# VectorE takes over the weighing of one-hots for odd blocks in every stage after the first

## The reference

```
x = x + attention(layernorm(x), ctx)          # 16 heads of 16, biases, softmax over 512 keys
x = x + experts(layernorm(x))
experts(x): x_norm = x * rsqrt(mean(x*x) + eps) * norm_w
            q   = x_norm @ wq                 # 8 heads x 2 halves x 128
            sim = q . keys                    # 64 scores per head and half
            top 16 of each half, top 16 of the 256 sums  -> 16 experts of 4096 per head, 128 per token
            hidden = gelu(x_norm . down[expert]) * relu(score)
            out    = sum over experts of hidden * up[expert]
```

## Time and profile before

| | |
|---|---|
| median of 3 runs | 1311.65 us (1310.05 to 1319.98) |
| profiled execution | 1311.6 us, span 1309.8 us |
| PE busy | 1086.9 us, 83% |
| DVE (VectorE) busy | 1038.1 us, 79% |
| POOL (GpSimd) busy | 588.6 us, 45% |
| ACT (ScalarE) busy | 394.9 us, 30% |

### The profile page before, as it was taken

One profiled execution on the slowest core, in us unless ns is written; L12 is line 12 of the kernel. 1 busy time (PEld: TensorE's weight loads), 2 busy tenths in 40 slices (PEclk: granted clock), 3 DMA queues, 4 the chain that ended last, 5 costly groups with the idle time before them and its releaser, 6 DMA issues.

```text
span 1309.8 us, 28838 instructions
## 1 busy us (share of the span) xinstructions
PE 1086.9 (83%) x10152; PEld 741.6 (57%) x10152; DVE 1038.1 (79%) x4899; ACT 394.9 (30%) x724; POOL 588.6 (45%) x708
## 2 busy tenths in 40 slices
PE   4799987887778862458889889998989898989998
PEld 2344442333213221357767778777878777768887
DVE  2657455959998998599999999999989999974621
ACT  1257544533334450122212222222222222222211
POOL 5230410513112123156766767666757575765500
PEclk9699998987879896559999989998999999989999
DMA  4344314221211101800000100010000010000000
GB/s 153 102 150 135 108 51 132 69 71 48 77 45 39 46 15 37 306 4 2 24 6 20 32 10 24 2 32 15 24 11 24 2 32 15 24 9 28 2 17 9
DMA packets 59924, 63.76 MB, mean 49 GB/s; under 512 B 6882, under 2 KB 56164, under 8 KB 59268
## 3 DMA queue, kind: packets, MB, share of 16 engines
q1 hardware_dynamic: 59780, 61.90, 14.8%
HBM read 42.21 MB, written 19.66 MB: 47 GB/s over the span
## 4 chain that ended last, share of the span: by engine, by line
DVE 38%; PE 24%; POOL 16%; issue 15%; DMA 3%; SPq 2%; ACT 2%; POOLq 0%; DVEq 0%; ACTq 0%
PE bank L1242 22%; POOL mem L774 5%; DVE mem L1199 4%; DVE mem L1165 4%; POOL mem L662 3%; DVE mem L1101 3%; DVE mem L1212 3%; PE bank L1245 2%; DVE mem L1084 2%; DVE mem L1097 2%; DVE mem L1104 2%; DVE mem L1196 2%; DVE mem L1048 2%; DVE mem L1047 2%; SPq L487 2%
## 5 line engine op out<-in xcount | busy, mean ns | idle before, releaser
L1242 PE MATMUL bank<-mem 128*128 128x32 bf16 (+5 forms) x9672 | 1037.4, 279 | 151.3 <-issue 60.9
L1242 PEld LDWEIGHTS bank<-mem 128*128 128x128 bf16 (+3 forms) x9672 | 689.3, 125 | 448.8 <-issue 227.6
L774 POOL TENSOR_TENSOR mem<-mem 128x1536 bf16<-128x1536 bf16 x118 | 326.4, 2767 | 249.2 <-DVE mem L1199 216.9
L1165 DVE TENSOR_REDUCE mem<-bank 128x1 f32<-128x512 f32 x256 | 167.8, 681 | 91.0 <-PE bank L1242 90.7
L874 ACT ACTIVATE mem<-bank 128x512 f32<-128x512 f32 x256 | 148.9, 601 | 207.3 <-PE bank L1242 206.4
L1212 DVE TENSOR_TENSOR mem<-mem 128x512 f32<-128x512 f32 x128 | 126.6, 989 | 80.9 <-ACT mem L911 73.5
L911 ACT ACTIVATE mem<-bank 128x512 f32<-128x512 f32 x128 | 76.5, 598 | 341.7 <-PE bank L1242 341.7
L1199 DVE TENSOR_TENSOR mem<-mem 128x2048 bf16<-128x2048 bf16 x128 | 158.9, 1241 | 0.0
L1245 PE MATMUL bank<-mem 128*128 128x128 f32 (+3 forms) x480 | 75.8, 289 | 68.3 <-POOL mem L693 25.0
L662 POOL TENSOR_TENSOR mem<-mem 128x32 f32<-128x32 f32 (+5 forms) x224 | 73.8, 364 | 117.8 <-DVE mem L1056 117.8
L920 ACT COPY mem<-bank 128x512 f32<-128x512 f32 x128 | 74.9, 586 | 160.5 <-PE bank L1242 160.5
(11 more groups left out here) (99 smaller groups left out, 729.2 us busy)
## 6 DMA issues: line engine op xcount, KB each, us to landing
mem<-parts_d SPq DMA_DIRECT2D x192, 64.0 KB, 2.2
parts_d<-mem SPq DMA_DIRECT2D x16, 384.0 KB, 2.6
mem<-in_L_ffn_expert_down SPq DMA_DIRECT2D x16, 256.0 KB, 3.0
downT_d<-mem SPq DMA_DIRECT2D x16, 256.0 KB, 3.1
mem<-downT_d SPq DMA_DIRECT2D x4, 1024.0 KB, 9.9
mem<-in_L_ffn_expert_up SPq DMA_DIRECT2D x4, 1024.0 KB, 17.3
tok_d<-mem SPq DMA_DIRECT2D x16, 160.0 KB, 1.8
mem<-tok_d SPq DMA_DIRECT2D x16, 160.0 KB, 2.5
```

Of the source, the lines that this page charges most:

```text
L774: nc.gpsimd.tensor_tensor(ow[q % 2], i0, i1, ALU.mult).then_inc(ow_rdy, 1)
L1165: nc.vector.tensor_reduce(nmx[g % 2][:, i % TB, i // TB:i // TB + 1], psum[n % 3][:, :], AX.X, ALU.max, negate=True).then_inc(s_max, 1)
L1242: return nc.tensor.matmul(o, l, r, start=first, stop=last)
```

## The change

In stages 0 to 6 VectorE weighs the blocks with odd q and GpSimd those with even q. Stage -1 keeps its division. That makes 56 weighings that move, 8 in each of seven stages. VectorE does its weighing right behind the one-hots of the same block and ahead of the tasks of the step. The address helper and the size are the same as before. `block_weighed` is rewritten to take stage and block apart, so that TensorE, VectorE and SyncE wait on the count to which a block now belongs; no wait is added to any of these queues, except that VectorE waits for its own low one-hots before it weighs them.

```diff
-        OWN = [q for q in range(16) if q % 3 != 0]
-        def block_weighed(eng, c):
-            if isinstance(c, int) and c in OWN:
-                eng.wait_ge(ow_own, OWN.index(c) + 1)
-            elif isinstance(c, int) and c < 16:
-                if c >= 0:
-                    eng.wait_ge(ow_rdy, c + 1 - sum(o < c for o in OWN))
-            else:
-                eng.wait_ge(ow_rdy, c + (1 - len(OWN)))
+        OWN_FIRST = [q for q in range(16) if q % 3 != 0]
+        OWN = [q for q in range(16) if q % 2 != 0]
+        def own(kk, q):
+            return q in (OWN_FIRST if kk == -1 else OWN)
+        def block_weighed(eng, slot, q):
+            if q < 0:
+                slot, q = slot - 1, q + 16
+            if isinstance(slot, int) and slot < 0:
+                return
+            if isinstance(slot, int) and slot == 0:
+                mine = sum(o <= q for o in OWN_FIRST)
+                first, more = mine, q + 1 - mine
             else:
+                mine = sum(o <= q for o in OWN)
+                first, more = len(OWN_FIRST) + mine - len(OWN), 16 - len(OWN_FIRST) + q + 1 - mine - (16 - len(OWN))
+            if own(-1 if isinstance(slot, int) and slot == 0 else 0, q):
+                eng.wait_ge(ow_own, first if isinstance(slot, int) and slot == 0 else slot * len(OWN) + first)
+            else:
+                eng.wait_ge(ow_rdy, more if isinstance(slot, int) and slot == 0 else slot * (16 - len(OWN)) + more)
...
# GpSimd's step
-                    if on(kk, -1, 6) and not (kk == -1 and q in OWN):
+                    if on(kk, -1, 6) and not own(kk, q):
                         weigh((k + 1) * 16 + q, par, q)
...
# VectorE's one_hots
-                block_weighed(dve, c - 2)
+                block_weighed(dve, k + 1, q - 2)
...
-                if kk == -1 and q in OWN:
+                if own(kk, q):
                     dve.wait_ge(oh_rdy, c * 2 + 1)
                     i0, i1 = weighing(q, tt)
                     nc.vector.tensor_tensor(ow[q % 2], i0, i1, ALU.mult).then_inc(ow_own, 1)
...
# TensorE's coefficients
-                block_weighed(pe, c)
+                block_weighed(pe, k + 1, q)
```

More of the change, by code:

```diff
@@ L575, in load_choice @@
                 if isinstance(tile, int):
-                    block_weighed(sp, (tile - 3) * BPT - 1)
-                    block_weighed(sp, (tile - 3) * BPT - 2)
+                    last = (tile - 3) * BPT - 1
+                    block_weighed(sp, last // 16, last % 16)
+                    block_weighed(sp, (last - 1) // 16, (last - 1) % 16)
                 sp.wait_ge(tok_wr, (tile + 1) * 16)
```

## The result

The changed kernel takes 1319.46 us (median of 5 runs, 1316.42 to 1324.21) against 1312.95 us for the kernel before on the same occasions (5 runs, 1310.05 to 1319.98). The ratio is 1.0054, 95% interval 1.0030 to 1.0078: half a per cent slower. The forecast was 1316.8 us, which is 1.0039 of the median of 1311.65 us that it was built on; the measured median is 2.7 us above it, and the measured ratio 0.0015. The profiled execution after takes 1316.4 us, span 1314.5.

What follows compares the result with a forecast made beforehand. The prediction took VectorE to bound stages 0 to 5, with TensorE not far behind. 41.3 - 26.9 - 2.6 - 5.3 - 3.3 + 2 = +5.2 us, on 1311.65 us, gave 1316.8 us, range 1306 to 1325.

Steps and rivals of the forecast that it cites:

- The bound: Stages 0 to 5: VectorE sets the pace, so added work is paid at once; in stage 6 it isn't.
- The added term: Stages 0 to 5: 48 weighings on VectorE at 0.86 us each, +41.3 us; the eight of stage 6 cost nothing.
- The holds by odd blocks: Stages 0 to 5: VectorE instructions stretched while GpSimd weighs odd blocks are no longer held, -26.9 us.
- The waits of `choose`: Three of ten waits for GpSimd's sums stand behind an odd weighing and go, -2.6 us; the long ones stay.
- The waits of `keys`: Four waits of 1.32 us for expert numbers that GpSimd starts late because of an odd weighing go, -5.3 us.
- Even weighings that start late: Where keys follow in an even step, the even weighing starts up to 1.3 us earlier: -3.3 us for four places.
- Disturbance: GpSimd's small operations run beside VectorE's one-hots more often, stretching them: +2 us, between 0 and +6.
- What was to be seen after: Profile: 66 and 62 weighings, multiply some 82 us, line 1084 about half, its waits gone, VectorE busy some 26 us more.
- sign of being wrong: Multiply's gelu waits over 10 us before stage 6, shrinking even holds, or a VectorE weighing clearly over 0.95 us.
- Rival 1: Stages 2 to 5: returned holds become waits for TensorE's gelus; 1337.5 us if all, 1327 if half; chance 0.2.
- Rival 2: GpSimd's free time shortens even holds too: 1304 us if half go, 1288 if all; chance 0.12.
- Rival 3: The port pair shared by VectorE and GpSimd is the bound: 91 us would go, to 1221 us; chance 0.02.

Runs made afterwards that it cites:

- the doubled weighing: Changed kernel plus a second, unused weighing of the same size before each VectorE weighing after stage -1: 1356.64 us in one run.
- the 52 blocks: Against the kernel before, VectorE weighs only 52 blocks of stages 0 to 5 whose GpSimd weighing held or delayed something: 0.9739, 1276.14 us.
- the account: Table over six profiled kernels: length of stages 0 to 5, holds, small stretches, idle, and price per moved weighing, 0.86 to 0.89 us.
- the slice: Kernel before with GpSimd weighing only 64 of 1536 elements per block after stage -1: 1239.93 us in one run.
- even -1.1%: VectorE weighs the even instead of the odd blocks in stages 0 to 6, against the kernel before: 0.9891, 1302.09 us.
- all -0.5%: VectorE weighs every block in stages 0 to 6 and GpSimd none, against the kernel before: 0.9952, 1305.30 us.
- its mirror image: VectorE weighs the other 44 blocks of stages 0 to 5, GpSimd all of stage 6, against the kernel before: 1.0278, 1350.67 us.

## Why the prediction was right, point by point

**The bound.** Right. In stages 0 to 5 VectorE paid every microsecond added (the doubled weighing) and kept every one returned (the 52 blocks). The moved weighings of stage 6 cost nothing: stages 6 and after are 0.8 us shorter.

**The added term.** 48 x 0.86 = 41.3; the account says 0.89 and 42.6. Right to 1.3 us.

**The holds by odd blocks.** -26.9, and the account has no hold by an odd block left. Right.

**The waits of `choose`.** Mis-sized: -2.6 forecast, 17.5 to 11.3 us measured, -6.2. I had said that the long waits all stand behind even blocks. The one of stage 1 stands behind block 3: 3.0 us more. The other 0.6 us are three short waits that stay and fall from 0.86 to 0.67 us.

**The waits of `keys`.** Mis-sized the other way: -5.3 forecast, 5.3 to 3.2 us measured. Only one of four went, that of stage 0, whose numbers stood behind odd block 11; the others fell from 1.32 to 1.06 us. Here the prediction read its rows wrongly. In these three places the weighing just before the numbers is an even one (block 12 of stage 1, block 6 of stages 2 and 4; in the earlier trace rows the one at 821.26), and it stays with GpSimd. The numbers still start 0.13 us ahead of VectorE's next high one-hots (825.11 and 825.24 in the earlier trace rows, 828.87 and 829.00 below). VectorE now has a weighing to do before it needs them, which alone would have shortened the wait by some 0.9 us, but GpSimd takes 0.7 us longer over them: the seven instructions of line 675 took 2.85 us in the earlier trace rows, and at the same place in stage 2, with VectorE's one-hots and weighing beside them, 3.57:

```profile
828.87 3.57 POOL L688 TENSOR_TENSOR mem<-mem 128x128 int32<-128x128 int32 x7
829.00 1.44 DVE L1212 TENSOR_TENSOR mem<-mem 128x2048 bf16<-128x2048 bf16 x1
830.36 1.06 DVE L1218 TENSOR_TENSOR mem<-mem 128x1536 bf16<-128x1536 bf16 x1
832.47 0.57 DVE L1097 SCALAR_TENSOR_TENSOR mem<-mem 128x400 f32<-128x400 f32 x1 [1.06 <-POOL mem L688]
```

**Even weighings that start late.** -3.3 forecast, -0.4 measured (31.7 to 31.3 us of holds by even blocks). A keys step is four two-input instructions in a row, and a weighing that misses the first catches the third, as at 896.40 above: in the timelines the even holds of the keys fell by only 2.4 us (14.4 to 12.0). Those of the multiply, which I had taken to stay, rose by 1.8 (14.4 to 16.2; the 15.5 of the prediction has some 1 us of smaller stretches in it).

**Disturbance.** +2 forecast; the small stretches fell by 1.9 us. What is booked here and what under the added term depends on the duration that is taken as unstretched; together the two terms were +43.3 forecast and +40.7 measured.

So the terms were off by +1.3, -3.6, +3.2, +2.9 and -3.9 us, and it is luck that these cancel: the sign and the size of the two large terms were read from rows, the small ones were right only in sum. By stage the forecast was about +4, near 0, and within 1 in each of the last four; measured are +3.0, -1.4, +2.5, -0.7, +2.5, -0.7. Stages 2 and 4 were missed by more than I had allowed: odd blocks return only some 4 us of holds there, against 6.4 in stages 3 and 5.

**What was to be seen after.** Right: 66 and 62 weighings, the multiply at 82.8 us (forecast 82), no gelu waits before stage 6. Wrong: the waits at the keys are not gone, those of `choose` are six and not seven, and VectorE's busy time rose by 14.8 us, not 26. In stages 0 to 5 it rose by 13.4, since instructions overlap a little, so that each weighing adds 0.89 and not 0.95 us, and since the small stretches fell. After them it rose by 1.4 and not by 7.6, since holds also fell in stage 6, where they cost nothing and I hadn't counted them. Line 1084 fell to less than half (24.3 to 10.4 us), but line 1088 took part of its holds. No sign of being wrong came: no gelu waits, even holds as they were, and a weighing of 0.975 us.

**The rivals.** Rival 1 (TensorE collects the gaps) did not happen; the slice shows where it would begin. Rival 2 (the even holds shrink too) did not: they kept their size. Rival 3, the port pair as the bound, did not: with all 96 weighings of stages 0 to 5 off GpSimd these stages take what they took before, 574.3 us.

**Slips that the sum did not feel.** The prediction put a weighing's cost to VectorE at up to 1.1 us, but the earlier trace rows has a multiply stretched by 1.9 us and line 1084 by 2.6, and the sum used the latter. It said that no row shows GpSimd's large operation waiting, though the earlier trace rows has a weighing of 3202 ns. An odd block is weighed 1.8 us sooner, not 1.9, by the two durations. And the chance of 0.11 for under 1298.5 us is more than its parts, half of rival 2 and rival 3, give (0.08).

## What to carry to other kernels

Moving work between VectorE and GpSimd is a trade per instruction, not per engine: each piece costs the bound engine its full time in the queue and returns what it had held or delayed there, which the timeline shows one by one, as long as that engine stays the bound. Moved by a regular rule the two sides cancelled here (odd +0.5%, even -1.1%, all -0.5%); the same kind of move, aimed by the list of holds, gave 2.6%, and its mirror image cost 2.8%. And look at the first step after a stage whose bound changes: work that was covered in the stage before can stand bare there.

## What the runs showed of the hardware

The hold works in both directions, where the prediction had a row for only one. A two-input instruction of VectorE waits for GpSimd's weighing to end (1.77 us instead of 0.67 in the earlier trace rows), and GpSimd's weighing, if it comes second, waits too: 3.43 us instead of 2.76 at 895.55 above. The Trainium skill, "SBUF — State Buffer", section "Who interferes with whom", says the same: whoever issues first keeps the shared pair for the whole instruction. By that, the trace agrees. Who comes first can't be read from the recorded starts to the last tenth: the weighing of 895.55 lost to line 1098 too, which starts at 895.80, for 895.55 + 0.67 = 896.22 is later than the end of line 1097 (895.88) and close to that of line 1098 (896.37).

Searches and maxima, which read one input, ran on beside weighings: 0.19 to 0.22 us each in stages 0 to 5 of the kernel before, under a weighing and away from one. One input is not always enough, though: line 1113, a `tensor_scalar` with one tensor input, took 1.19 us under a weighing instead of 0.23.
